# An attention and feed-forward layer in split fp32r on one core: the standing matmul buffers moved to four distances from the moving ones

## What is computed

```python
xn = _layernorm(x, axis=-1)
# attention
q = (xn @ Wq + bq) + pe ; k, v = split(xn @ Wkv + bkv) ; k = k + pe
probs = softmax(where(causal, q @ k.T * scale, min))      # 8 heads, one k and v
attn = (probs @ v) @ Wo
# feed-forward
xr, xk = mu_r*xn + (1-mu_r)*xn_prev , mu_k*xn + (1-mu_k)*xn_prev
ffn = sigmoid(xr @ W_r.T) * (square(relu(xk @ W_k.T)) @ W_v.T)
out = x + attn + ffn
```

## Time and profile before

| | before |
|---|---|
| median of 3 runs | 1515.31 us (1510.8 to 1518.69) |
| span of the profiled execution | 1512.0 us |
| PE busy | 1484.7 us (98%), 11724 matmuls |
| weight loads (PEld) | 1448.2 us (96%) |
| DVE, ACT, POOL busy | 84%, 70%, 76% |
| granted TensorE clock | mean 0.998 of full |

### The profile page before, as it was taken

How to read it: one execution, slowest core, us unless ns; L and a number is a source line. 1 busy time by engine, 2 the same in 40 slices (tenths; PEclk the granted TensorE clock), 3 DMA queues, 4 the chain that set the end, 5 groups by cost and what they waited for, 6 DMA issues and landing times.

```text
span 1512.0 us, 36188 instructions
## 1 busy us (share of the span) xinstructions
PE 1484.7 (98%) x11724; PEld 1448.2 (96%) x11724; DVE 1262.6 (84%) x3424; ACT 1052.6 (70%) x2531; POOL 1153.7 (76%) x1665
## 2 busy tenths in 40 slices
PE   7999999999999999999999999999999999999998
PEld 6999999999999999999999999999999999999998
DVE  7988869888698896988879888788887988879875
ACT  5777667776677766767677676767767776777764
POOL 6787777787777787877778777778777787778774
PEclk9999999999999999999999999999999999999999
DMA  4144422444224542344423444134441344413453
GB/s 129 44 126 135 132 87 67 116 141 141 74 69 119 146 137 60 86 120 139 128 58 96 120 137 136 43 100 122 137 139 38 105 130 138 138 29 101 127 153 105
DMA packets 225801, 164.39 MB, mean 109 GB/s; under 512 B 51792, under 2 KB 220880, under 8 KB 225616
## 3 DMA queue, kind: packets, MB, share of 16 engines
q1 hardware_dynamic: 224768, 161.69, 37.1%
q10 hardware_dynamic: 848, 0.40, 0.1%
HBM read 81.27 MB, written 77.59 MB: 105 GB/s over the span
## 4 chain that ended last, share of the span: by engine, by line
PE 75%; DVE 10%; DMA 7%; SPq 3%; issue 3%; ACT 1%; POOL 1%; DVEq 0%; ACTq 0%; POOLq 0%
PE pS L1036 26%; PE pO L1173 21%; PE pG L1036 12%; PE pG L1123 8%; PE pT L1139 7%; DMA park_dram<-Y 5%; SPq L455 3%; DVE X L1015 2%; DVE mix L861 1%; DMA Z<-park_dram 1%; DVE Y L924 1%; DVE pt L940 1%; DVE qtmp L850 1%; PE pS L1123 1%; DVE xn L810 1%
## 5 line engine op out<-in xcount | busy, mean ns | idle before, releaser
L766 ACT ACTIVATE X<-X,bias 128x16 f32<-128x16 f32 (+56 forms) x512 | 376.0, 734 | 156.3 <-DVE bias L1015 154.8
L1036 PE MATMUL pS<-kt,qt 128*128 128x288 f32 (+41 forms) x2304 | 462.2, 329 | 4.1 <-DVE kv L837 2.5
L1173 PE MATMUL pO<-pt,v 128*128 128x256 f32 x3288 | 435.4, 283 | 2.5 <-DVE ot L994 2.4
L1173 PEld LDWEIGHTS pO<-pt,v 128*128 128x128 f32 x3288 | 399.8, 189 | 3.6 <-DVE ot L994 3.4
L575 POOL TENSOR_SCALAR X<-X,rec 128x16 f32<-128x16 f32 (+56 forms) x512 | 373.6, 730 | 26.9 <-DVE rec L914 16.2
L1015 DVE CUSTOM_DVE_ANT_0 X<-pS,mask 128x16 f32<-128x16 f32 (+56 forms) x512 | 353.7, 691 | 40.8 <-PE pS L1036 33.9
L1036 PEld LDWEIGHTS pS<-kt,qt 128*128 128x128 f32 x2304 | 365.2, 189 | 16.8 <-issue 3.7
L542 POOL TENSOR_TENSOR pt<-Z,pt 128x256 fp32r<-128x256 f32 (+5 forms) x192 | 317.7, 1655 | 78.7 <-ACT pt L688 77.8
L527 POOL TENSOR_TENSOR qt<-qtmp,qt 128x256 fp32r<-128x256 f32 x252 | 194.5, 772 | 62.8 <-ACT qt L661 55.2
L940 DVE TENSOR_TENSOR pt<-pT,pt 128x512 fp32r<-128x512 f32 (+3 forms) x440 | 207.7, 493 | 37.9 <-ACT pt L695 37.1
L759 ACT CAST ot<-pO 128x256 fp32r<-128x256 f32 x256 | 95.9, 375 | 173.4 <-PE pO L1173 94.3
(11 more groups left out here) (118 smaller groups left out, 1943.4 us busy)
## 6 DMA issues: line engine op xcount, KB each, us to landing
park_dram<-Y SPq DMA_DIRECT2D x32, 512.0 KB, 2.6
Z<-park_dram SPq DMA_DIRECT2D x128, 128.0 KB, 3.0
park_dram<-Y SPq DMA_DIRECT2D x32, 448.0 KB, 3.2
Z<-park_dram SPq DMA_DIRECT2D x128, 112.0 KB, 2.7
park_dram<-Y SPq DMA_DIRECT2D x32, 384.0 KB, 2.9
Z<-park_dram SPq DMA_DIRECT2D x128, 96.0 KB, 2.5
park_dram<-Y SPq DMA_DIRECT2D x32, 320.0 KB, 2.9
Z<-park_dram SPq DMA_DIRECT2D x128, 80.0 KB, 2.2
```

The costliest lines, as they stand in the source:

```text
L766: nc.scalar.activation(x_row(s, 0, w), x_row(s, 0, w), ACT.Exp, bias=bias[:, j:j + 1], scale=-1.0, accum_out=total[:, j:j + 1]).then_inc(e ...
L1036: last = nc.tensor.matmul(out, a[i], m[j], start=start and k == 0, stop=stop and k == n - 1)
L1173: last = nc.tensor.matmul(pO[:, 0:2 * P], v[i][:, k, :], pt[j][:, pair % 2, k, :], start=n == 0, stop=n == 3 * nk - 1)
```

## The change

Three gaps of 32 bytes take the place of the one of 64, and the buffers are put in another order. No instruction is added, removed, moved or resized; the order of all engines is as before. `wr` goes to the moving buffers at 0. Then come `wq` and `kh` at 32, `wkv` and `ot` at 64, and `wk`, `qt`, `v` and `vs` at 96.

```diff
--- before.py
+++ after.py
@@ -240,16 +240,18 @@
         kt = [sb(f"kt{i}", [P, T], R) for i in range(2)]
         pt = [sb(f"pt{i}", [P, 2, NT, 2 * P], R) for i in range(2)]
         wo = [sb(f"wo{i}", [P, H, E], R) for i in range(2)]
-        gap = sb("gap", [P, 16])
+        wr = [sb(f"wr{i}", [P, CT, E], R) for i in range(2)]
+        gap0 = sb("gap0", [P, 8])
         wq = [sb(f"wq{i}", [P, CT, H * D], R) for i in range(2)]
+        kh = [sb(f"kh{i}", [P, CT, CHUNK], R) for i in range(2)]
+        gap1 = sb("gap1", [P, 8])
+        wkv = [sb(f"wkv{i}", [P, CT, 2 * D], R) for i in range(2)]
+        ot = [sb(f"ot{i}", [P, H, P], R) for i in range(2)]
+        gap2 = sb("gap2", [P, 8])
         wk = [sb(f"wk{i}", [P, CT, E], R) for i in range(2)]
-        wkv = [sb(f"wkv{i}", [P, CT, 2 * D], R) for i in range(2)]
-        wr = [sb(f"wr{i}", [P, CT, E], R) for i in range(2)]
-        kh = [sb(f"kh{i}", [P, CT, CHUNK], R) for i in range(2)]
         qt = [sb(f"qt{i}", [P, 2, CHUNK // SUB, H, SUB], R) for i in range(2)]
         v = [sb(f"v{i}", [P, NT, D], R) for i in range(2)]
         vs = sb("vs", [P, TPC, D], R)
-        ot = [sb(f"ot{i}", [P, H, P], R) for i in range(2)]
         bq = sb("bq", [P, H])
         mu = sb("mu", [P, 4])
         omu = sb("omu", [P, 4])
```

## The result

The changed kernel takes 1526.41 us, the median of 4 runs (1524.54 to 1528.28), against 1513.89 us for the kernel before beside it (1510.8 to 1518.69): a ratio of 1.0076, with a 95% interval of 1.0046 to 1.0106. It is slower by 12.5 us.

What follows compares the result with a forecast made beforehand. PE's own matmul stream was taken to set the time. Terms summed as 1512.0 + 0 + 0 = 1512 us, 3.3 us below the median of the runs, so the forecast median was 1516 us, with 8 in 10 from 1501 to 1538.

Steps and rivals of the forecast that it cites:

- no change: Whole kernel: placement leaves PE's pace as it was, around 1516 us, own range 1508 to 1523; chance 0.43.
- the slower rival: Values, Q and feed-forward streams of 256 columns: load clashes with stream, all fills at longer pace, +12 us, 1527; chance 0.36.
- Neither end has a row that favours it; I take zero: Fills of 256 columns: moving between two paces bounded at 12 us each way, counted as zero.
- Does the distance slow the moving stream? Nothing: Right half of the scores: departures of +0.5, +0.2 and -4 ns per matmul at 0, 32 and 96, taken as nothing.
- the part on what the rows can't show: At 256 columns stream and load are almost equally long, so how they fall together could choose the pace.
- Does it slow the weight load?: Loads in scores and transposes: 188, 187, 188 ns at 0, 32, 96, and 141 for transposes; nothing.
- The price of a step, 4 ns on half of 6032 matmuls, +12 us,: Matmuls of 256 columns with changed distance: half assumed at each pace, shifting between them costs or saves 12 us.
- a third pace: All 6032 matmuls of 256 columns one step slower still: +36 us, 1551, the tail of the slower case.
- The two paces of the earlier trace: Two output projection fills of 24 matmuls at distance 64, read as 117.4 and 121.3 ns per interval.
- The faster rival: Fills of 256 columns at 32 or 96 bytes all take the shorter pace: -12 us, 1504; chance 0.21.
- The tiles behind: Tiles shifted 32 bytes later, used by DVE, ACT, POOL and DMAs: no term, as DVE has 16% left.
- the change doing what it says: Buffer allocation: gaps are exactly the 32-byte allocation unit, so distances come out as planned; the contrary rival got no chance.

Runs made afterwards that it cites:

- e6: TensorE alone, layer left out: streams of 24 matmuls of 128 to 512 columns at distances 0, 32, 64 and 96; settled paces 111.7 to 234.6 ns.
- the map: TensorE alone, layer left out: 24 matmuls of 256 columns at distances 0 to 496 bytes in steps of 16; 113.3 ns at 64, 120.0 at 0.
- e1: Kernel before with its gap of 64 bytes left out, standing buffers at distance 0: 1538.69 us, ratio 1.0159.
- e7: TensorE alone, buffers placed as in the kernel before, each product as 24 matmuls of 256 columns, four times: 113.3 or 117.8 ns.
- e11: TensorE alone, layer left out: 256 columns at distances 44 to 84 in steps of 4, and 32, 96, 192, eight entries each; at 64 113.3 or 117.8 ns.
- e12: Kernel before with all standing buffers carved from one tile so every distance is 76 bytes modulo 256: 1508.66 us against 1515.93, ratio 0.995.
- e4: Changed kernel's buffer order with one gap of 64 bytes instead of three of 32, FR at 0: 1516.18 us, ratio 1.0011 to the kernel before.

## Why the prediction was right or wrong

**What bounds the kernel** was right: only the pace of PE counted. Of the 13.8 us of span 11 are PE busy time. The other 2.8 are idle time, in which one wait grew by 6.4 us and others shrank.

**The forecast had no change as the likeliest case, at 1516 us, and that did not come; the time came out where the slower rival had it** (1527 forecast, 1526.4 measured), inside the stated range of 1501 to 1538. The step that failed is "Neither end has a row that favours it; I take zero". I had seen two paces at one distance and concluded that "the distance is not what sets them there". The runs say that both count. At 0, 32 and 96 no fill of the values or of Q settled at the short pace, at 64 in the kernel before 86 of 184 fills of the values did, and what ran ahead picks which. That costs 13.0 to 23.7 us for a kernel with one gap at 96, 32 or 0. The kernel before stood at a favourable place, from which all four moves to 0, 32, 96 and 192 led down and one, to 76, led up.

**The mechanism that the slower rival named,** a load in the way of the stream or held by it, is shown in part only. That the pace goes by the place of the two operands to each other is shown; that it is the load's reading that meets the stream's is not. And it doesn't show "only where stream and load are equally long": at 448 and 512 columns the distances differ too.

**"Does the distance slow the moving stream? Nothing"** was read from widths of 320 to 416. At 320 and 384 columns it holds (e6: within 1.3 ns), but the rows of 400 and 408 grew by 4 and 5 ns in the changed kernel. It could not bear on 256, as the part on what the rows can't show said. I then still gave no change the greatest chance on the strength of rows that I had called blind. The four classes were also sorted modulo 128. Modulo 256 the widths 352 and 416 stood at 192, and 344 and 408 at 224.

**"Does it slow the weight load?"** Nearly right: in the map loads have 187 to 190 ns at all distances but 0, where they have 192 (in e1 too), and those of the transposes stay at 141. The rows of loads at distance 0 that I read, 188 ns, were from streams of 400 columns.

**The price of a step, 4 ns on half of 6032 matmuls, +12 us,** was the right size by errors that cancel, which is luck. Fewer were short than half (44% of the values and 40% of Q, hardly any of FR and FK). But the intervals that had been long grew as well: those of the values above 115 ns went from 117.8 to 118.7 in the mean, since fills at 120 came in, a third pace that I had only as a tail. By the means of the table the 6032 account for 12.8 us. KV and WO, for which I had no term since their distance stays, changed too: KV won 38 points of short share (-0.6 us) and WO lost 17 (+1.2 us). That other fills now run ahead of them is the likely reason, and not shown.

**The two paces of the earlier trace rows** were read as 117.4 and 121.3 ns with a slow first interval in both. Without that first one, of 202 to 204 ns, the two fills run at 113.3 and 117.8 ns: the two settled paces of e7 and e11.

**The faster rival** did not come at 32 or 96. Its door exists, though: e12 went through it.

**The tiles behind, and the change doing what it says:** no term, as forecast; e4 to e1 rule them out.

**Beside the rule of the Trainium skill** (TensorE: Matmul & The Clock Gate, step-by-step part): two independent read ports, so that a load takes nothing from the running matmul. The measurement decides against it as a rule that placement can't matter for the time. With the same loads and streams and nothing else running, the pace is 113.3 or 120.0 ns by the distance alone. The estimate from the same page, 109 ns at 256 columns, is 4 ns under the pace at 64 bytes and 11 under that at 0. Whether it is the ports or something behind them no run tells.

## What to carry to other kernels

Where every matmul has a weight load of its own and its stream is about as long as the load (here 256 columns against a load's pace of 112 ns), the distance of standing and moving fp32r buffers modulo 256 bytes is worth a look, with a map measured with TensorE alone. It took one kernel of 400 us, and between the worst and the best place tried lie 2% of this kernel. The map is a guide and no proof: in the full kernel it missed the short fills at 192 and the slow FR at 76, so try the place in the kernel itself. Read starts, not durations: two paces 4.5 ns apart hide in one mean of 283 ns. And where a trace shows two paces for the same work, find out what picks one before calling the cause hidden.

## What was not expected of the hardware

- The period is 256 bytes, and within it the short pace of 113.3 ns sits at 52, 64 and 76, with 117.8 to 119.8 at 56, 60, 68 and 72 between them.
- At 64 a fill of equal matmuls has two settled paces, 113.3 and 117.8 ns, and keeps one to its end. What ran ahead picks it: in e7 the width of one matmul, 64 columns against 272, 288 or 304, made the difference for five of the six products at 64.
- In the map of 256 columns a weight load lasts 192 ns at distance 0 and 187 to 190 at all others.
- Streams of 512 columns run at 226.7 ns at distance 0, one of the slowest places at 256 columns, and at 233.3 to 234.6 at the other three. The cause is open, as is that of the short fills at 192 in the full kernel.
- Why the pace repeats every 256 bytes no run shows.
